# VectorE's order within a pair of attention steps: masks, sinks, small operations and lowests in pairs

## What is computed

```python
x = x + tanh(g_xattn) * attention(layernorm(x), ctx)
#   score = q k / 4 * mask; score = where(score == 0, -1e9, score); softmax; times v; @ wo + bo
x = x + tanh(g_ffn) * experts(layernorm(x))
#   top 2 of 4 by router logits; softmax over them; each expert: (silu(x w1) * (x w3)) w2
```

## Time and profile before

| | |
|---|---|
| runs, median (lowest to highest) | 489.86 us (488.34 to 490.08) |
| profiled execution | 489.78 us, span 487.8 us |
| TensorE busy | 460.8 us (94% of the span) |
| VectorE busy | 378.9 us (78%) |
| ScalarE busy | 306.6 us (63%) |
| GpSimd busy | 196.2 us (40%) |
| chain that ended last | TensorE 67%, VectorE 16%, ScalarE 5%, issue 4%, GpSimd 3% |
| mean granted clock of TensorE | 0.987 |

### The profile page before, as it was taken

One profiled execution on the slowest core, in us unless ns is written; L12 is line 12 of the kernel. 1 busy time (PEld: TensorE's weight loads), 2 busy tenths in 40 slices (PEclk: granted clock), 3 DMA queues, 4 the chain that ended last, 5 costly groups with the idle time before them and its releaser, 6 DMA issues.

```text
span 487.8 us, 11552 instructions
## 1 busy us (share of the span) xinstructions
PE 460.8 (94%) x3720; PEld 433.3 (89%) x3720; DVE 378.9 (78%) x876; ACT 306.6 (63%) x768; POOL 196.2 (40%) x204
## 2 busy tenths in 40 slices
PE   7799898988878999999999999999999999999995
PEld 5578786877767999899999999999999999999895
DVE  2577996879964788986888888888878878878772
ACT  2435556364335667686767757767777767776783
POOL 4528695498784035252136253113303303302312
PEclk9989999999979999999999999999999999999999
DMA  8529998842012204042023132022112112102211
GB/s 259 158 54 397 381 405 322 338 149 90 24 54 102 67 22 87 4 91 24 23 25 66 46 68 44 23 46 24 34 34 44 17 27 33 22 13 34 23 13 23
DMA packets 33968, 45.22 MB, mean 93 GB/s; under 512 B 10183, under 2 KB 30613, under 8 KB 33685
## 3 DMA queue, kind: packets, MB, share of 16 engines
q1 hardware_dynamic: 25999, 35.21, 21.4%
q0 software_dynamic: 6576, 8.92, 10.9%
q10 hardware_dynamic: 1344, 0.48, 0.5%
HBM read 32.91 MB, written 21.82 MB: 112 GB/s over the span
## 4 chain that ended last, share of the span: by engine, by line
PE 67%; DVE 16%; ACT 5%; issue 4%; POOL 3%; ACTq 1%; DMA 1%; DVEq 0%; SPq 0%; POOLq 0%
PE ps_rows L1751 22%; PE ps_wide L1771 7%; PE ps_probT L1751 7%; PE ps_misc L1771 7%; PE ps_wide L1585 5%; DVE w_lo L1396 3%; PE ps_misc L1607 2%; PE ps_misc L1539 2%; PE ps_rows L1800 2%; DVE w_lo L1392 2%; PE ps_wide L1811 1%; PE ps_probT L1565 1%; PE ps_rows L1553 1%; DVE score L1306 1%; DVE ps_rows L1401 1%
## 5 line engine op out<-in xcount | busy, mean ns | idle before, releaser
L1219 POOL DMA_INDIRECT out_x<-y_out,meta x35 | 64.1, 1830 | 190.9 <-ACT y_out L1018 185.8
L1396 DVE TENSOR_TENSOR w_lo<-w,w_hi 128x512 fp32r<-128x512 f32 x152 | 104.1, 685 | 13.4 <-issue 6.7
L1751 PE MATMUL ps_rows<-xt_hi,w_hi 128*128 128x256 f32 x384 | 110.6, 288 | 0.2 <-DVE xt_lo L1410 0.2
L1751 PE MATMUL ps_rows<-xt_lo,w_hi 128*128 128x256 f32 x384 | 108.6, 283 | 0.0
L1751 PE MATMUL ps_rows<-xt_hi,w_lo 128*128 128x256 f32 x384 | 108.6, 283 | 0.0
L967 ACT CAST w_hi<-w 128x512 fp32r x152 | 95.2, 627 | 4.4 <-issue 4.0
L1751 PEld LDWEIGHTS ps_rows<-xt_hi,w_hi 128*128 128x128 f32 x384 | 73.5, 191 | 0.4 <-DVE xt_lo L1410 0.4
L1751 PEld LDWEIGHTS ps_rows<-xt_lo,w_hi 128*128 128x128 f32 x384 | 73.7, 192 | 0.0
L1751 PEld LDWEIGHTS ps_rows<-xt_hi,w_lo 128*128 128x128 f32 x384 | 73.6, 192 | 0.0
L981 ACT ACTIVATE act_g<-ps_rows 128x256 f32<-128x256 f32 x96 | 37.3, 389 | 28.7 <-PE ps_rows L1751 23.9
L996 ACT CAST hid_hi<-ps_rows 128x256 fp32r<-128x256 f32 x96 | 36.1, 376 | 27.3 <-DVE ps_rows L1401 26.4
(11 more groups left out here) (241 smaller groups left out, 1160.2 us busy)
## 6 DMA issues: line engine op xcount, KB each, us to landing
grouped<-in_pad SPq DMA_DIRECT2D x1, 10296.0 KB
w<-in_L_ffn_w SPq DMA_DIRECT2D x8, 1024.0 KB, 12.3
w2s<-in_L_ffn_w SPq DMA_DIRECT2D x4, 1024.0 KB, 13.8
xg<-grouped SPq DMA_DIRECT2D x16, 256.0 KB, 2.7
out_x<-xall SPq DMA_DIRECT2D x8, 256.0 KB, 5.1
xall<-in_x SPq DMA_DIRECT2D x1, 1024.0 KB, 12.0
xall<-in_x SPq DMA_DIRECT2D x1, 768.0 KB, 7.4
ctxT<-in_ctx_t SPq DMA_DIRECT2D x2, 308.0 KB, 5.2
```

Of the source, the lines that this page charges most:

```text
L1219: pool.indirect_dma_start(out, bass.IndirectOffsetOnAxis(ap=meta[:, s % 2, t, E:E + 1].bitcast(U32), axis=0), y_out[:, s % 2, t, :], None, ...
L1396: dve.tensor_tensor(w_lo[:, f % NB], unit_weights(e, f), w_hi[:, f % NB].bitcast(F32), ALU.subtract).then_inc(w_lo_done, 1)
L1751: mm = pe.matmul(ps_gu[f % NB][:, m, 0:n], lhs, rhs[:, a, c, 0:n], start=(k == 0), stop=(k % (3 * DC) == 3 * DC - 1), skip_group_check=True)
```

## The change

VectorE's body now goes by pairs: both masks; then, for the first pair, `residual(b-2)`; in body 2 `off_mean(2)`; in a BEGIN body statistics and variance; in a FINAL body `invert`; then both sinks, the inversion of the denominators, the slots' small operations, in a FOLLOW body all five routing functions; then both lowests; and, in bodies that are not BEGIN, the statistics last. In body 1 the last four tiles' sums stand in the first pair, the variance in the second. ScalarE waits for the last mean ahead of the norm of batch 4 instead of ahead of body 2. No instruction is added or removed.

```diff
--- before.py
+++ after.py
@@ -824,6 +824,8 @@
                     if isinstance(b, int) and b < 2:
 
                         act.wait_ge(mean_off_done, b + 1)
+                    if b == X_PARTS[-1][0]:
+                        act.wait_ge(mean_off_done, len(X_PARTS))
                     if after_first(b):
 
                         act.wait_ge(xT_done, b)
@@ -953,7 +955,6 @@
                 body(0, first=True)
                 body(1)
 
-                act.wait_ge(mean_off_done, len(X_PARTS))
                 for b in range(2, B - 1):
                     body(b)
                 body(B - 1, last=True)
@@ -1318,43 +1319,43 @@
                     dve.reciprocal(rden[:, g], weighed[:, b % 2, QT * g:QT * (g + 1), :, DH]).then_inc(rden_done, 1)
 
                 def body(b):
-                    for s in range(NS):
-                        if s % QT == 0:
-                            for t in range(QT):
-                                mask_scores(b, s + t, False)
-                        if isinstance(b, int) and b == 1:
-
-                            if s < 2:
-                                sums(2, NT - 4 + 2 * s, NT - 2 + 2 * s)
-                            elif s == 2:
+                    for g in range(DC):
+                        pair = range(QT * g, QT * (g + 1))
+                        for s in pair:
+                            mask_scores(b, s, False)
+                        if g == 0 and b > 1:
+                            residual(b - 2)
+                        if b == 1:
+                            if g == 0:
+                                sums(2, NT - 4, NT)
+                            else:
                                 variance_of_x(2)
-                            else:
-                                off_mean(2)
-                        if s == 0 and b in FINAL:
+                        if (b, g) == (2, 0):
+                            off_mean(2)
+                        if g == 0 and b in BEGIN:
+                            batch_stats(dve, b - 2)
+                            variance2(dve, BEGIN[b])
+                        if g == 0 and b in FINAL:
                             invert(dve, FINAL[b])
-                        if s == 1 and b in BEGIN:
-                            variance2(dve, BEGIN[b])
-                        sink_zeros(b, s)
-                        if s % QT == 0:
-                            invert_sums(b - 1, s // QT)
-                        find_lowest(b, s)
-                        if s == 0 and b > 1:
-                            residual(b - 2)
-                            batch_stats(dve, b - 2)
-                        if (b, s) == (B - 2, 0):
+                        for s in pair:
+                            sink_zeros(b, s)
+                        invert_sums(b - 1, g)
+                        if (b, g) == (B - 2, 0):
                             hand_out(dve, 0)
-                        if (b, s) == (B - 2, 1):
                             hand_out_begin(dve, 0)
                             hand_out_owner(dve, 0)
-                        if (b, s) == (B - 1, 1):
+                        if (b, g) == (B - 1, 0):
                             hand_out_rest(dve, 0)
-                        if s == 2 and b in FOLLOW:
+                        if g == 1 and b in FOLLOW:
                             logit(dve, FOLLOW[b])
                             compare(dve, FOLLOW[b])
                             order_of(dve, FOLLOW[b])
-                        if s == 3 and b in FOLLOW:
                             choose(dve, FOLLOW[b])
                             lag(dve, FOLLOW[b])
+                        for s in pair:
+                            find_lowest(b, s)
+                        if g == 0 and b > 1 and b not in BEGIN:
+                            batch_stats(dve, b - 2)
 
                 for i in range(2):
                     sums(i, *(QT * b for b in X_PARTS[i]))
```

## The result

The changed kernel takes 497.81 us (median of four runs, 497.65 to 498.99) against 489.95 for the kernel before in the same set: ratio 1.0174, interval 1.0150 to 1.0197. It is 8 us slower. The forecast was 493.5 and its range ended at 497.0: the direction is right, the size is half of what came. The profiled span is 495.7 us, 7.9 more than before; the mean granted clock 0.981 instead of 0.987.

A forecast was written before the change was run, and what follows sets the result against it. TensorE was taken to bound the kernel, its few waits on VectorE and GpSimd mattering. Terms 0.3 + 2.3 - 0.45 - 0.35 + 1.9 = +3.7 us on 489.86 gave 493.5 us, range 491.0 to 496.5, 489.0 to 497.0 with rivals taken in.

The forecast's parts named there:

- Bound and direction: Whole kernel: TensorE's own work sets the expert half, so a shift at 160 us reaches the end whole; +3.7 us, slower.
- Batches 1 to 4: The residual's 0.56 us wait goes, but batch 1's paired sinks meet GpSimd's bias: +0.3 us (-0.6 to +0.9).
- Batch 5: Gates wait behind the residual and project_o(3), so the second norm TensorE waits for comes late: +2.3 us (+1.4 to +3.2).
- Gates begin at T + 2.65: Batch 5: GpSimd's gates start 2.65 us after project_o(3) ends, at 99.2, 2.9 us later than before.
- Slower still: Rival: longer waits in batches 5 and 7 bring one more lower-clock stretch, 2.2 us: 495.7 us or 496.6; chance 0.12.
- Batch 6: Routing ahead of the lowests removes a hindrance: logits -0.45 us (-0.75 to +0.7), wait for chosen experts -0.35 (-0.5 to 0).
- my bound of -0.75: Batch 6 logits: the gain if all hindrance between VectorE's routing operations and GpSimd is gone.
- nobody reads them before the experts: Batch 6: GpSimd's scatters move behind the later lowers; no cost was charged for that.
- The -0.35 for the choice: Batch 6: TensorE's 0.5 us wait for the chosen experts shrinks as choose follows the order at once (-0.5 to 0).
- Batch 7: GpSimd's chain from gates to context starts later, after project_o(5), delaying TensorE's transpose of context: +1.9 us (+1.3 to +2.8).
- T + 13.2: Batch 7: TensorE's transpose of context comes 13.2 us after project_o(5) ends; before it was 11.3 us.
- gates at T + 2.65: Batch 7: GpSimd's gates start 2.65 us after project_o(5) ends.

The follow-up runs named there:

- the run with slots late: Changed kernel with the slots' small operations (hand_out and its followers) behind the lowests in batches 6 and 7: 497.81 us, ratio 1.0178.
- invert first: Changed kernel with invert ahead of the residual in batches 5 and 7: 496.61 us, ratio 1.0155.
- the best order alone: Changed kernel with residual, its statistics and the slots' operations behind the lowests, and batch 6's last scatters ahead of lower 2: 487.49 us, ratio 0.9952.
- the run with the fill: Changed kernel with 12 matmuls on zeros in TensorE's wait for the second norm in batch 5: 496.93 us, ratio 1.0140.

## Why the prediction was half right

**Bound and direction: right.** The shift at the first expert matmul reaches the end whole (7.79 of 7.9 us), and it comes from batches 5 and 7.

**Batches 1 to 4: right.** The residual's wait at 54.10 is gone; 0.68 us of shift at project_o(3) stands against the term of 0.3 with a bound of 0.9, and 0.46 of it was there ahead of the first residual.

**Batch 5: the mechanism right, the size 2.75 for 2.3.** "Gates begin at T + 2.65": measured 99.79 - 97.21 = 2.58. The first of them took 1.34 us beside the sinks where 0.72 stood before. The Trainium skill's SBUF — State Buffer, Who interferes with whom, lets a GpSimd operation that comes second wait for VectorE's two-input one to its end; the trace agrees, and with back-to-back sinks the wait is nearly their whole 1.48 us.

**The step that failed most:** the sum put one more stretch at the lower clock at nothing. It stood only as the rival *Slower still*, "bring TensorE to the lower clock earlier or once more", at 2.2 us and 0.12. In the profiled execution it came in batch 5 and cost 1.60 us. The other terms of the ledger add up to 0.68 + 2.75 - 0.12 + 2.91 = 6.2 us, or 496.0 us, which the range still holds. What brings the stretch on stays open, since the run with slots late has the same wait without it; but a forecast that lengthens TensorE's waits, when the earlier trace rows show the clock at 0.50 behind one, has to put a price for it into the sum.

**Batch 6: the logits right in kind, a new wait missed.** The logits' wait fell by 0.73 us, my bound of -0.75 rather than -0.45: the operation that took 1598 ns at most takes 169 at most now. But "nobody reads them before the experts" failed: nobody reads the scatters, yet the context of batch 5 is queued behind them on GpSimd. That is the 1.05 us, a term that the sum put at nothing. The -0.35 for the choice is matched by -0.44 up to project_o(5), in which it lies with other work.

**Batch 7: +2.91 for +1.9, just over the bound of 2.8.** The steps gave T + 13.2 for the context; with T = 136.25 the transpose came at T + 14.20. The step that failed is "gates at T + 2.65": they came at T + 3.35. It let GpSimd wait for VectorE's reciprocal, as it did for 2.25 us in batch 5 before. Now GpSimd came to the gates straight from its work of batch 6, at 139.58. The reciprocal was ready no sooner (139.50), because the variance's small operation met a lower of GpSimd and took 0.93 us instead of 0.17; but with invert first, where it was ready 4.5 us ahead, the gates still came only behind that work. The first gate again took 1.40 beside the sinks. VectorE and GpSimd in batch 7 of the kernel after:

```profile
138.28 0.93 DVE L327 TENSOR_SCALAR vareps<-mv 128x4 f32<-128x4 f32 x1
...
139.32 0.18 DVE L440 RECIPROCAL total<-total 128x4 f32<-128x4 f32 x1
```

```profile
137.94 1.23 POOL L1142 TENSOR_TENSOR score<-score,lowest 128x616 f32<-128x616 f32 x1
139.12 0.46 POOL L1130 TENSOR_TENSOR kblock<-kT,small 128x154 f32<-128x154 f32 x1
139.60 1.40 POOL L446 TENSOR_SCALAR share<-total,tanh_g 128x4 f32<-128x4 f32 x1
```

The terms of the ledger against the forecast: +0.4 on batches 1 to 4, +0.45 on batch 5's norm, +1.60 clock, +0.7 for batch 6 (-0.73 + 1.05 - 0.44 = -0.12 against -0.80), +1.0 on batch 7: 4.1 us of what was missing, which takes 3.7 to 7.8.

## What to carry to other kernels

An operation that waits for another engine should not stand ahead of ready work on an engine that executes in order: list what is queued behind it, and do the same for every engine which that work feeds, GpSimd's DMA issues included, since they delay the operations behind them even when nobody reads their data. When a change lengthens a wait of TensorE, look up in the trace what its clock does around such waits and what a stretch at the lower clock costs, and put that into the sum with a chance; look for the stretch in more than one execution before naming its cause. Where a wait cannot be shortened, idle matmuls in it can be worth as much as a better order: here 2.5 us in the kernel before (ratio 0.9947; the best order alone 0.9952).

## What the runs showed that was not expected

- The granted clock can be held through a wait of about 2 us by matmuls on zeros alone: in batch 7 it was 1.00 from 140 to 148 us with 17 of them, where it was 0.57 without. A clock of 1.00 is the 2.4 GHz level.
- A stretch at the lower clock need not follow a long wait: the one from 39 us in the run with the fill came when TensorE's longest wait since 26 us had been 0.74 us.
- A four-element GpSimd operation that meets two sinks back to back takes 1.34 to 1.40 us in the kernel after, and 0.27 where it meets none (the run with invert first).
- Of the ten runs of the kernel with pairs, slots and scatters moved, the faster ones show the higher mean granted clock: 483.60 us at 0.994, 488.38 at 0.988.
- Profiled executions differ by up to 1.7 us by batch 5 before anything has changed in them: TensorE's transpose of the first lowered scores there starts at 103.98 in the kernel after and at 105.65 in the run with the fill, which is the same program up to that point; the stretch at the lower clock from 39 us in the latter accounts for most of this. Shifts are therefore read from mark to mark, not from the start.
